# A shared FFN of an eighth batch beside the experts, and a merge of a float16 pair one round later

## The reference

```python
x = x + cross_attention(layernorm(x), ctx)      # 16 heads of 128 over 8 key/value heads, 256 context rows
h = layernorm(x)                                # 4096 rows
topk_idx, topk_w = gate(h)                      # 4 of 32 experts for each row, within 2 of 4 groups
out = 0
for e in range(32):                             # at most CAP = 128 rows for each expert
    out[rows_e] += topk_w * (silu(h[rows_e] @ w1[e]) * (h[rows_e] @ w3[e])) @ w2[e]      # 512 -> 256 -> 512
shared = (silu(h @ shared_gate) * (h @ shared_up)) @ shared_down                         # 512 -> 512 -> 512
x = x + out + shared
```

## Time and profile before

| | |
|---|---|
| median of three timed runs | 1661.3 us (1658.97 to 1665.91) |
| the profiled execution | 1658.14 us, its span 1656.4 us |
| granted TensorE clock, mean | 0.993 |
| busy, share of the span | PE 97%, PE weight loads 70%, DVE 73%, ACT 50%, POOL 49% |
| attention | up to about 1355 us |
| pieces and routing behind it | about 1355 to 1412 us |
| 32 expert rounds | about 1412 to 1634 us |
| last adds | to 1656.4 us |

### The profile page before, as it was taken

How to read it: one execution, slowest core, us unless ns; L and a number is a source line. 1 busy time by engine, 2 the same in 40 slices (tenths; PEclk the granted TensorE clock), 3 DMA queues, 4 the chain that set the end, 5 groups by cost and what they waited for, 6 DMA issues and landing times. The chain is left out here.

```text
span 1656.4 us, 34806 instructions
## 1 busy us (share of the span) xinstructions
PE 1613.0 (97%) x12194; PEld 1152.5 (70%) x12194; DVE 1213.3 (73%) x3508; ACT 820.0 (50%) x2028; POOL 819.9 (49%) x1136
## 2 busy tenths in 40 slices
PE   7999999999999999999999999999999999999994
PEld 5767677777777776867777767777777777655541
DVE  7987676767677676767676877787877766677782
ACT  5764343434344434434443544545454433677782
POOL 2444544546363546454454555546464447344443
PEclk9999999999999999999999999999999999999997
DMA  8753433334443433334343554555454467599984
GB/s 252 181 144 77 87 77 85 84 66 96 78 97 62 94 71 84 77 79 81 81 84 73 114 78 105 98 116 106 92 108 83 98 217 238 166 281 293 298 262 65
DMA packets 394477, 204.12 MB, mean 123 GB/s; under 512 B 347824, under 2 KB 356016, under 8 KB 394304
## 3 DMA queue, kind: packets, MB, share of 16 engines
q1 hardware_dynamic: 380432, 180.27, 44.8%
q0 software_dynamic: 13312, 20.57, 6.4%
q10 hardware_dynamic: 560, 1.05, 0.2%
HBM read 87.15 MB, written 31.36 MB: 72 GB/s over the span
## 5 line engine op out<-in xcount | busy, mean ns | idle before, releaser
L959 ACT ACTIVATE arena<-arena,neg_max 128x256 f32<-128x256 f32 x512 | 253.7, 496 | 379.2 <-DVE neg_max L1266 379.2
L696 POOL TENSOR_SCALAR arena<-arena,prob_scale 128x256 f16<-128x256 f32 x384 | 183.9, 495 | 452.4 <-DVE prob_scale L1275 444.1
L1617 PE MATMUL ps_query<-xn_both,arena 128*128 128x256 f16 x1024 | 279.1, 273 | 1.8 <-DMA xn_both<-xn_half 1.8
L1618 PE MATMUL ps_query<-xn_both,arena 128*128 128x256 f16 x1024 | 279.1, 273 | 0.0
L1619 PE MATMUL ps_query<-xn_both,arena 128*128 128x256 f16 x1024 | 279.1, 273 | 0.0
L1266 DVE CUSTOM_DVE_ANT_0 arena<-ps_score,mask_add 128x256 f32<-128x256 f32 x512 | 186.5, 420 | 126.1 <-PE ps_score L1619 126.0
L1281 DVE SCALAR_TENSOR_TENSOR arena<-arena,prob_scale 128x256 f16<-128x256 f32 x384 | 233.8, 656 | 7.1 <-POOL arena L696 7.1
L1617 PE MATMUL ps_out<-arena,o_t 128*128 128x512 f16 x512 | 194.1, 379 | 2.1 <-DVE o_t L1286 2.1
L1618 PE MATMUL ps_out<-arena,o_t 128*128 128x512 f16 x512 | 194.0, 379 | 0.0
L1619 PE MATMUL ps_out<-arena,o_t 128*128 128x512 f16 x512 | 194.0, 379 | 0.0
L751 POOL DMA_INDIRECT slot_table<-entry,slot_at x128 | 133.9, 1046 | 48.1 <-issue 33.6
(11 more groups left out here) (325 smaller groups left out, 4058.1 us busy)
## 6 DMA issues: line engine op xcount, KB each, us to landing
arena<-w SPq DMA_DIRECT2D x96, 512.0 KB, 7.3
x_in<-x SPq DMA_DIRECT2D x15, 512.0 KB, 3.9
xn_rows<-xn_half SPq DMA_DIRECT2D x15, 512.0 KB, 3.1
out_rows_dram<-x SPq DMA_DIRECT2D x30, 256.0 KB, 2.3
ctx_in<-ctx_t SPq DMA_DIRECT2D x16, 256.0 KB, 3.0
weight_in<-wq SPq DMA_DIRECT2D x8, 512.0 KB, 5.5
weight_in<-wo SPq DMA_DIRECT2D x8, 512.0 KB, 4.5
arena<-arena SPq DMA_TRANSPOSE x256
```

Source lines behind the costliest of these rows:

```text
L696: pool.tensor_scalar(p_rows[:, c, 0, :], probs[:, c, :], prob_scale[:, c:c + 1], 1.0, ALU.mult, ALU.mult).then_inc(norm_hi, 1)
L959: act.activation(probs[:, c, :], probs[:, c, :], ACT.Exp, bias=neg_max[:, c:c + 1], scale=-1.0, accum_out=prob_sum[:, c:c + 1]).then_inc(e ...
L1617: pe.matmul(dst, a.hi, b.hi, start=start and n == 0, stop=False)
L1618: pe.matmul(dst, a.hi, b.lo, start=False, stop=False)
```

## The change

The batches from 8 on are deferred instead of those from 9 on, so eight are in `LATE`, four of them kept in DRAM. `BESIDE` gives a piece to each of the rounds 0 to 23. The pieces behind the experts all use `ps_fill[0]`; `ps_query` becomes the second bank for the products of even experts (`y_bank`), beside `ps_out[0]`. `add_in` has three places: iterations 4 (batch 3 of `LATE`), 14 (4 and 5) and 24 (6 and 7).

The merge takes two float16 products: the matching matrix, now float16, by the high and the low part of the unmerged products of `e + 1`, scaled by `PAIR_S / EY_S`. `pair_high` (ScalarE) and `pair_rest` (VectorE) make the parts in even rounds, in the tile `o_t`, free by then. `match` moves from even rounds to odd ones, and loses a cast. `merge(e - 3)` stands in odd rounds behind `expert_up`, so one round later than before. `scale_y(e - 1)` moves to the end of ScalarE's even round, `scale_y(e - 3)` to the end of its odd round. `expert_rows(e + 2)` stands ahead of `expert_hidden(e)`. The loops run one round longer. The diff without its repeats (declarations, the counts of `KEPT`, calls of `piece_bank`) and without context:

```diff
@@ -43,6 +43,8 @@
+PAIR_S = 16.0
@@ -50,8 +52,9 @@
-DEFER = 9
-LATE = (9, 10, 14, 15, 11, 12, 13)
+DEFER = 8
+LATE = (8, 9, 14, 15, 10, 11, 12, 13)
+KEPT = len(LATE) - 4
@@ -63,7 +66,7 @@
-    if _e % 8 != 7 and EARLY + len(BESIDE) < len(PIECES):
+    if EARLY + len(BESIDE) < len(PIECES):
@@ -255,10 +258,11 @@
-        pair_match = [one_hot[:, :, :, :].rearrange("p t k e -> p (t k e)")[:, n * P:(n + 1) * P] for n in range(2)]
+        pair_match = [one_hot[:, :, :, :].rearrange("p t k e -> p (t k e)").bitcast(F16)[:, n * P:(n + 1) * P]
+                      for n in range(2)]
+        pair_y = o_t
...
-        row_f, to_spare, hits, row_moved = scratch[:, 0:E], scratch[:, E:2 * E], scratch[:, 2 * E:2 * E + 1], \
-            scratch[:, 2 * E + 1:2 * E + 2]
+        row_f, to_spare, hits = scratch[:, 0:E], scratch[:, E:2 * E], scratch[:, 2 * E:2 * E + 1]
@@ -269,7 +273,15 @@
-        ps_piece = [ps_fill[0], ps_query]
+        def piece_bank(k):
+            return ps_query if k % 2 and k < EARLY else ps_fill[0]
+        def y_bank(e):
+            return ps_out[1] if e % 2 else (ps_out[0], ps_query)[e // 2 % 2]
@@ -432,7 +444,8 @@
-        add_in = {e + e % 2: (n - 1, n) for n in (4, 6) for e, k in BESIDE.items() if PIECES[k] == ("d", n, TB - 1)}
+        add_in = {max(e + e % 2, 4): ns for ns in ((3,), (4, 5), (6, 7)) for e, k in BESIDE.items()
+                  if PIECES[k] == ("d", ns[-1], TB - 1)}
@@ -1006,7 +1019,7 @@
             def scale_y(e):
...
-                    act.wait_ge(pe_ey, e + 1)
+                    act.wait_ge(pair_lo, e // 2 + 1)
@@ -1014,7 +1027,13 @@
-                act.activation(expert_y[e % 6], ps_out[e % 2][:, :], ACT.Copy, scale=1.0 / EY_S).then_inc(scaled_y, 1)
+                act.activation(expert_y[e % 6], y_bank(e)[:, :], ACT.Copy, scale=1.0 / EY_S).then_inc(scaled_y, 1)
+            def pair_high(e):
+                act.wait_ge(pe_ey, e + 1)
+                if e > 1:
+                    act.wait_ge(pe_merged, e // 2)
+                act.activation(pair_y.hi, y_bank(e)[:, :], ACT.Copy, scale=PAIR_S / EY_S).then_inc(pair_hi, 1)
@@ -1095,7 +1114,7 @@
-                    scale_y(e - 1)
+                    pair_high(e - 1)
@@ -1104,10 +1123,12 @@
-                if e >= 2 and e % 2 == 0:
-                    scale_y(e - 2)
...
+                if e >= 2 and e % 2 == 0:
+                    scale_y(e - 1)
+                if e >= 3 and e % 2:
+                    scale_y(e - 3)
@@ -1421,19 +1442,22 @@
             def match(e):
...
-                dve.wait_ge(pe_eht, e + 1)
+                dve.wait_ge(pe_eht, e + 2)
...
-                dve.tensor_scalar(pair_match[m % 2], ps_head[:, FB * P:(FB + 1) * P], row_f[:, e + 1:e + 2], EY_S,
+                dve.tensor_scalar(pair_match[m % 2], ps_head[:, FB * P:(FB + 1) * P], row_f[:, e + 1:e + 2], EY_S / PAIR_S,
...
-                dve.scalar_tensor_tensor(row_moved, hits, to_spare[:, e + 1:e + 2], row_f[:, e + 1:e + 2], ALU.mult,
-                                         ALU.add).then_inc(*own.up())
-                dve.wait_ge(*own.now())
-                dve.tensor_copy(second_rows[:, m:m + 1], row_moved).then_inc(matched, 1)
+                dve.scalar_tensor_tensor(second_rows[:, m:m + 1], hits, to_spare[:, e + 1:e + 2], row_f[:, e + 1:e + 2],
+                                         ALU.mult, ALU.add).then_inc(matched, 1)
+            def pair_rest(e):
+                dve.wait_ge(pair_hi, e // 2 + 1)
+                dve.scalar_tensor_tensor(pair_y.lo, y_bank(e + 1)[:, :], PAIR_S / EY_S, pair_y.hi, ALU.mult,
+                                         ALU.subtract).then_inc(pair_lo, 1)
@@ -1586,7 +1610,7 @@
-            dve.tensor_scalar(to_spare, row_f, spare_row[:, 0:1], -1.0 / EY_S, ALU.subtract, ALU.mult).then_inc(
+            dve.tensor_scalar(to_spare, row_f, spare_row[:, 0:1], -PAIR_S / EY_S, ALU.subtract, ALU.mult).then_inc(
@@ -1603,8 +1627,10 @@
-                if e < E and e % 2 == 0:
-                    match(e)
+                if e >= 2 and e % 2 == 0:
+                    pair_rest(e - 2)
+                if e < E and e % 2:
+                    match(e - 1)
@@ -1699,8 +1725,10 @@
             def piece(k):
...
-                ps = ps_piece[k % 2]
-                if k >= 2:
+                ps = piece_bank(k)
+                if k > EARLY:
+                    pe.wait_ge(*piece_emptied(k - 1))
+                elif k >= 2:
@@ -1799,32 +1827,36 @@
-                    pe.wait_ge(matched, (e + 1) // 2)
+                    pe.wait_ge(matched, e // 2)
...
-                if e % 2 == 0:
+                if e % 2:
...
-                    columns.append(row_f[:, e:e + 1].broadcast_to([P, P]))
+                    columns.append(row_f[:, e - 1:e].broadcast_to([P, P]))
...
             def expert_down(e):
...
-                if e >= 2:
+                if e < 2:
+                    pe.wait_ge(x1_done, TB * B)
+                elif e % 2:
...
+                elif e == 2:
+                    pe.wait_ge(*piece_emptied(EARLY - 1))
...
-                    pe.wait_ge(x1_done, TB * B)
+                    pe.wait_ge(scaled_y, scaled_at(e - 4))
...
-                products(ps_out[e % 2][:, :], [(expert_h_t[e % 2][:, f, :], w[:, f * D:(f + 1) * D])
+                products(y_bank(e)[:, :], [(expert_h_t[e % 2][:, f, :], w[:, f * D:(f + 1) * D])
...
             def merge(e):
...
-                pe.wait_ge(scaled_y, scaled_at(e + 1))
-                pe.matmul(ps_out[0][:, :], pair_match[e // 2 % 2], expert_y[(e + 1) % 6], start=False, stop=True).then_inc(
-                    pe_merged, 1)
+                pe.wait_ge(pair_lo, e // 2 + 1)
+                pe.matmul(y_bank(e)[:, :], pair_match[e // 2 % 2], pair_y.hi, start=False, stop=False)
+                pe.matmul(y_bank(e)[:, :], pair_match[e // 2 % 2], pair_y.lo, start=False, stop=True).then_inc(pe_merged, 1)
@@ -1881,19 +1913,19 @@
-            for e in range(E + 1):
+            for e in range(E + 2):
...
+                if e >= 3 and e % 2:
+                    merge(e - 3)
...
-                if e >= 1:
+                if 1 <= e <= E:
...
+                if e + 2 < E:
+                    expert_rows(e + 2)
...
-                if e + 2 < E:
-                    expert_rows(e + 2)
-                if e >= 2 and e % 2 == 0:
-                    merge(e - 2)
```

More of the change, by code:

```diff
@@ L117, in build @@
         xn2_rows = nc.dram_tensor("xn2_rows", (N + CAP, 2 * D), F16, kind="Internal").ap()
-        x2t_kept = nc.dram_tensor("x2t_kept", (3, P, 2 * KD * T), F16, kind="Internal").ap()
+        x2t_kept = nc.dram_tensor("x2t_kept", (KEPT, P, 2 * KD * T), F16, kind="Internal").ap()
         slot_table = nc.dram_tensor("slot_table", (CAP * E, 2), U32, kind="Internal").ap()
@@ L287, in build @@
         out_x2t = signal("out_x2t")
-        in_x2t = [signal(f"in_x2t{n}") for n in range(3)]
+        in_x2t = [signal(f"in_x2t{n}") for n in range(KEPT)]
         added_first, added = signal("added_first"), signal("added")
@@ L318, in build @@
         dve_own, pool_own = signal("dve_own"), signal("pool_own")
-        matched, pe_merged = signal("matched"), signal("pe_merged")
+        matched, pe_merged, pair_hi, pair_lo = (signal(n) for n in ("matched", "pe_merged", "pair_hi", "pair_lo"))
         CONSTS = 14
@@ L526, in load_x2t @@
             def load_x2t(n):
-                sp.wait_ge(out_x2t, 48)
+                sp.wait_ge(out_x2t, 16 * KEPT)
                 sp.wait_ge(pe_up, ups(n - 4, FSB))
@@ L608, in sync_program @@
                 load_expert(e)
-                if AHEAD - 1 <= e < AHEAD + 2:
+                if AHEAD - 1 <= e < AHEAD - 1 + KEPT:
                     load_x2t(e - AHEAD + 5)
-            sp.wait_ge(out_x2t, 48)
+            sp.wait_ge(out_x2t, 16 * KEPT)
             sp.wait_ge(out_rows, 16 * TB * B)
@@ L1211, in piece @@
                     return
-                u, ps = ups(n, f), ps_piece[k % 2]
+                u, ps = ups(n, f), piece_bank(k)
                 dve.wait_ge(tanhed, u + 1)
```

## The result

The changed kernel takes 1652.4 us in the median of nine runs (1645.24 to 1656.56), the kernel before 1661.3 us in nine beside them (1658.25 to 1667.75): ratio 0.9941 with a 95% interval of 0.9925 to 0.9957. It is faster by 0.6%, 9 us. The forecast was 1647 us, the range 1638 to 1657. The profiled execution took 1653.46 us.

What follows compares the result with a forecast made beforehand. TensorE was taken to bound up to round 20, then a serial chain of DMA landings. Last shared adds at 1587.7 + 11.3 + 32.0 + 11.7 = 1642.7 us span; plus 1.7 and 3.2 gives 1647.6, said as 1647; range 1638 to 1657.

Runs made afterwards that it cites:

- the early scalings: ScalarE's scalings of expert rows moved forward in the changed kernel: 1652.2 us, 0.9945; added to the kernel with back-to-back adds (1649.3 us): 1645.1 us.
- the best kernel: Changed kernel with each pair's adds back to back, gathers behind them except in iterations of shared adds, scalings moved forward: 1645.1 us, ratio 0.9895.
- the merge alone: Changed kernel with batches, pieces and shared adds placed as before, so only the float16 merge is new: 1661.8 us against 1660.7, ratio 1.0012.
- the batch alone: Kernel before with eight deferred batches and shared adds in iterations 4, 14 and 24, old float32 merge kept: 1649.6 us, ratio 0.9933.

## What to carry to other kernels

Where a serial queue of DMA landings sets the end, price a change by the queue: for each entry, when it is ready, when it is issued and how long it lands under the load of that place; time that TensorE gained ahead of it was worth nothing here. Check that the queue has caught up before you build its next step from the producer's time, and shorten the queue's own step (here by taking the gather out from between a pair's two adds) before you speed up the producer: the early scalings gave nothing with a backlog and 4.2 us without one. Whatever else is issued on that queue, as the gathers here, goes ahead of the blocking wait.

## What was unexpected of the hardware

An indirect accumulating DMA of 128 rows of 2 KB lands in 4.1 to 5.0 us near the end of the changed kernel (68 GB/s from 1608 to 1616 us), and in 4.4 to 10.7 us in the rounds of its two profiles (325 GB/s in the pair shown). The four shared adds took up to 12.6 us to land there (12.3 in the best kernel, from 1586.06 to 1598.34; 12.6 with the merge alone).

Executions of nearly the same program reached round 0 up to 5 us apart, and 9.5 us with the one on another chip, though the granted clock in attention was 1.00 in each profile. Part of the spread arises in the first turn. SyncE's second load of `x` starts at 30.2 to 31.8 us in the seven profiles whose granted clock over the first 20 us was 1.00, at 31.5 to 32.5 us in the four at 0.91, and at 33.7 to 34.0 us in the three at 0.85 or 0.86. It isn't all: of two profiles with that load at 33.7 us, one starts round 0 at 1396.9 and one at 1398.9. Between 200 us and round 0, TensorE waited 3.9 us for the transposes into `arena` in the changed kernel, and 0.5 us in the batch alone.
